# A two-layer decoder in one program: attention cores in chunks of four heads, and three-product scores and output projection in the second cross-attention

## The reference

```python
# self-attention, both layers (first cross-attention alike, no mask, keys of ctx: 1024)
scores = jnp.einsum('bhqd,bhkd->bhqk', q, k) / math.sqrt(dh)
scores = jnp.where(causal, scores, jnp.finfo(jnp.float32).min)
probs = jax.nn.softmax(scores, axis=-1)
attn = jnp.einsum('bhqk,bhkd->bhqd', probs, v)
...
# second cross-attention: H = 16 heads of D = 128, context split at N_IMG = 257
q = rms_norm(x @ q_w + q_b, nq_s).reshape(B, S, H, D)
k_txt = rms_norm(txt_ctx @ k_w + k_b, nkt_s).reshape(B, -1, H, D)
v_txt = (txt_ctx @ v_w + v_b).reshape(B, -1, H, D)
out_txt = sdpa(q, k_txt, v_txt)
k_img = rms_norm(img_ctx @ ki_w + ki_b, nki_s).reshape(B, -1, H, D)
v_img = (img_ctx @ vi_w + vi_b).reshape(B, -1, H, D)
out_img = sdpa(q, k_img, v_img)
out = (out_txt + out_img).reshape(B, S, INNER)
return out @ o_w + o_b
```

## Time and profile before

| | us |
|---|---|
| median of 3 runs | 3690.84 (3683.32 to 3691.17) |
| profiled execution: time | 3685.6 |
| profiled execution: span | 3683.8 |

### The profile page before, as it was taken

The page is one execution under the profiler, slowest core; times in us unless marked ns, Lnnn a source line. Parts: engine busy times, 40 slices in busy tenths (PEclk is TensorE's granted clock), DMA queues, the critical chain, the costliest instruction groups (busy, mean ns, idle before and its releaser), DMA issues. The chain is left out here.

```text
span 3683.8 us, 40622 instructions
## 1 busy us (share of the span) xinstructions
PE 3145.7 (85%) x13163; PEld 1907.7 (52%) x13166; DVE 1262.7 (34%) x1863; ACT 966.9 (26%) x2096; POOL 835.5 (23%) x819
## 2 busy tenths in 40 slices
PE   7699796988549786888996998999999856999997
PEld 3354342333548633446885884555554442777773
DVE  3133334564401212435434225555552131111114
ACT  1133033554101012323332004444442000222220
POOL 2100001100121101002442104555553013212215
PEclk9656897999669986659998999999999957999998
DMA  2132203331059612313443433222220000999996
GB/s 77 44 80 58 88 12 76 71 76 31 28 183 325 225 62 58 81 47 123 140 142 114 133 99 132 71 71 72 71 71 20 24 18 16 340 334 338 338 332 190
DMA packets 320633, 442.93 MB, mean 120 GB/s; under 512 B 45502, under 2 KB 179622, under 8 KB 320520
## 3 DMA queue, kind: packets, MB, share of 16 engines
q1 hardware_dynamic: 290056, 370.14, 32.4%
q0 software_dynamic: 15488, 44.09, 3.8%
q10 hardware_dynamic: 14976, 27.27, 2.1%
HBM read 308.78 MB, written 75.58 MB: 104 GB/s over the span
## 5 line engine op out<-in xcount | busy, mean ns | idle before, releaser
L1360 PE MATMUL ps<-moe_blocks_xgt,moe_blocks_w 128*128 128x128 f32 (+1 forms) x3072 | 364.0, 277 | 8.8 <-DMA moe_blocks_b1s<-rb_cols 5.5
L510 ACT ACTIVATE normed<-ps 128x512 f32<-128x512 f32 (+3 forms) x512 | 247.5, 516 | 463.7 <-PE ps L452 293.3
L1360 PEld LDWEIGHTS ps<-moe_blocks_xgt,moe_blocks_w 128*128 128x128 f32 (+1 forms) x3072 | 348.9, 183 | 16.6 <-issue 15.0
L2239 POOL TENSOR_TENSOR normed<-normed,xa_core_rinv 128x257 f32<-128x257 f32 (+1 forms) x256 | 266.2, 1062 | 273.0 <-DVE xa_core_rinv L2170 273.0
L1342 PE MATMUL ps<-moe_blocks_w,moe_blocks_ht 128*128 128x512 f32 (+1 forms) x624 | 284.9, 593 | 0.0
L2206 ACT ACTIVATE normed<-ps,xa_core_nmax 128x257 f32<-128x257 f32 (+1 forms) x256 | 173.8, 685 | 321.8 <-DVE xa_core_nmax L2165 321.4
L2116 PE MATMUL ps<-xa_core_k,xa_core_q 128*128 128x512 f32 x512 | 242.3, 596 | 14.1 <-DVE xa_core_k L2155 11.4
L2165 DVE TENSOR_REDUCE xa_core_nmax<-ps 128x1 f32<-128x257 f32 (+1 forms) x256 | 164.5, 683 | 250.1 <-PE ps L2116 250.1
L1431 DVE COPY moe_blocks_y<-ps 128x512 f32<-128x512 f32 x104 | 72.0, 692 | 459.9 <-PE ps L1342 436.3
L2142 PE MATMUL ps<-xa_core_pt,xa_core_v 128*128 128x512 f32 x512 | 225.1, 592 | 0.7 <-DVE xa_core_pt L2178 0.7
L559 DVE TENSOR_REDUCE xa_core_nmax<-ps 128x1 f32<-128x1024 f32 x128 | 156.0, 1224 | 139.9 <-PE ps L432 139.9
(11 more groups left out here) (290 smaller groups left out, 5263.7 us busy)
## 6 DMA issues: line engine op xcount, KB each, us to landing
moe_blocks_w<-L_ffn_rw SPq DMA_DIRECT2D x80, 704.0 KB
...
sa_core_packed<-sa_core_parts SPq DMA_DIRECT2D x384, 64.0 KB
...
```

What stands on the lines that cost most here:

```text
L510: nc.scalar.activation(probs[:, e % RING, a:S], g.ps[:, 4 + h, a:S], ACT.Exp).then_inc(exp_done, 1)
L1360: mm = nc.tensor.matmul(g.ps[0:fn, 2 + s % 2 + 2 * half, f * P:(f + 1) * P], w1s[s][:, k, half * F + f0:half * F + f0 + fn], xgt[:, s % 2, ...
L2239: ins = nc.gpsimd.tensor_tensor(prob[:, n % PR, lo:hi], prob[:, n % PR, lo:hi], rinv[:, n % PR, m:m + 1].to_broadcast([P, hi - lo]), ALU.mult)
```

## The change

`attention_core` works on NI = 8 chunks of four heads instead of 16 pairs. The high and low parts of a chunk go to DRAM in one DMA (`spill`), and six DMAs of 32 partitions x 4 heads bring them back packed (`pack`, 1.5 MB for a self-attention chunk, 2.25 MB for a cross-attention chunk); rows go in by two DMAs. The packed tensors have three slots (`pq`, `pk`). Values are stored plainly, [P, B, kt, D]; PE multiplies four heads of 32 columns into one bank and, with `g.ones`, the four sums into another, so that nothing has to be laid out: `lay` is gone, ACT takes both banks and DVE divides in the middle of the maxima of the next chunk. Both heads' score products now come ahead of both mask products. The maxima of chunk i + 1 are spread as EACH = 3 groups per key block of chunk i.

In the second cross-attention, keys are scaled by their gain at the projection (a second activation per unit), and queries are stored as high and low parts; the reciprocal for queries is one per token row (`rq` is [P, NT]) and comes into maximum and exponential as a scale. In the core GpSimd scales the keys, ACT and DVE split them, PE makes each score product as three float32r products (`split_matmul`) and a quarter of the values of the head before in every step. Keys have one raw buffer and are loaded ahead of the values. `output_cross1` is new: heads outside, the eight token tiles inside over eight banks, three products each.

```diff
-    NI, NP, QB = B * KC, B * KC * HPC // 2, S // P
-    NK = nkt * P
-    KB = NK // S
-    SLOTS = 4
+    NI, QB = B * KC, S // P
+    KB = nkt * P // S
+    SLOTS = 3
     PB = 2 if causal else 1
-    RING = 8
+    STEPS = 2
     TERMS = ((0, 0), (1, 0), (0, 1))
     KR = len(TERMS) * DH
-    PACK = 16 * 2 * 2 * len(TERMS)
+    PACK = 16 * 2 * len(TERMS)
+    PCS = HPC * QB // 2 if causal else HPC * QB
+    EACH = -(-PCS // (nkt - 1))
...
+            def spill(i):
+                sp.wait_ge(low_done, 2 * i + 2)
+                sp.dma_start(parts_dram[i], parts[i % PB][:, :, :].bitcast(F32)).then_inc(spilled[i % 2], 16)
+
+            def pack(i):
+                s = i % SLOTS
+                sp.wait_ge(spilled[i % 2], 16 * (i // 2 + 1))
+                if i >= SLOTS:
+                    sp.wait_ge(st_made, HPC * nkt * (i - SLOTS + 1))
+                t = parts_dram[i].rearrange("(h p) a n -> p h a n", p=DH)
+                for r, (qp, kp) in enumerate(TERMS):
+                    sp.dma_start(pq[r * DH:(r + 1) * DH, s, :, :].bitcast(F32),
+                                 t[:, :, qp, :]).then_inc(packed_in[s], 16)
+                    sp.dma_start(pk[r * DH:(r + 1) * DH, s, :, :].bitcast(F32),
+                                 t[:, :, 2 + KB * kp:2 + KB * (kp + 1), :].rearrange("p h a n -> p h (a n)")
+                                 ).then_inc(packed_in[s], 16)
+
+            def put_rows(i):
+                sp.wait_ge(row_low, i + 1)
                 for n in range(2):
-                    for h in range(2):
-                        sp.dma_start(packed[KR + n:KR + n + 1, j % SLOTS, h, 0, :].bitcast(F32),
-                                     rows[h * QB:(h + 1) * QB, j % 2, n, :].bitcast(F32)).then_inc(rows_in[j % 2], 16)
-
-            def lay(j):
-                i = j // 2
-                sp.wait_ge(taken, j + 1)
-                if j % 2 == 0 and i >= 1:
-                    sp.wait_ge(normed, i)
-                for h in range(2):
-                    a = (2 * (j % 2) + h) * DH
-                    val, ones = (3 if h else 0) * DH, (1 + h) * DH
-                    sp.dma_start(ot[a:a + DH, i, :], osb[val:val + DH, j % 2, :]).then_inc(spread[j % 2], 16)
-                    sp.dma_start(total[a:a + DH, :], osb[ones:ones + DH, j % 2, :]).then_inc(spread[j % 2], 16)
-
-            for j in range(SLOTS):
-                pack(j)
+                    sp.dma_start(pq[KR + n:KR + n + 1, i % SLOTS, :, :].bitcast(F32),
+                                 rows[:, i % 2, n, :].bitcast(F32)).then_inc(rows_in[i % 2], 16)
...
+            spill(0)
+            spill(1)
+            pack(0)
+            pack(1)
             put_rows(0)
-            for j in range(NP):
-                if j >= 1 and j + SLOTS - 1 < NP:
-                    pack(j + SLOTS - 1)
-                if j + 1 < NP:
-                    put_rows(j + 1)
-                if j >= 1:
-                    lay(j - 1)
-            lay(NP - 1)
-            for n in range(2):
-                sp.wait_ge(spread[n], 64 * NP // 2)
+            for i in range(NI):
+                if i + SLOTS - 1 < NI:
+                    spill(i + SLOTS - 1)
+                    pack(i + SLOTS - 1)
+                if i + 1 < NI:
+                    put_rows(i + 1)
...
+            def values(i, kb):
+                step, a = nkt * i + kb, start_of(kb)
+                b, c = divmod(i, KC)
+                pe.wait_ge(exp_done, HPC * step + HPC)
+                if kb == 0 and i >= 1:
+                    pe.wait_ge(taken, 2 * i)
+                for h in range(HPC):
+                    nc.tensor.matmul(g.ps[h * DH:(h + 1) * DH, 6, a:S], v[:, b, kb, c * P + h * DH:c * P + (h + 1) * DH],
+                                     probs[:, HPC * (step % STEPS) + h, a:S], start=(kb == 0), stop=(kb == nkt - 1))
+                for h in range(HPC):
+                    mm = nc.tensor.matmul(g.ps[h * DH:(h + 1) * DH, 7, a:S], g.ones[:, 0:DH],
+                                          probs[:, HPC * (step % STEPS) + h, a:S], start=(kb == 0), stop=(kb == nkt - 1))
+                mm.then_inc(pv_made, 1)
...
+            for i in range(NI):
                 for kb in range(nkt):
-                    scores(j, kb, 0)
-                    scores(j, kb, 1)
-                    if kb == 0 and j + 1 < NP:
-                        turn(j + 1)
+                    ahead = range(min(PCS, EACH * kb), min(PCS, EACH * (kb + 1))) if i + 1 < NI else ()
+                    if i == 0:
+                        for m in ahead:
+                            piece(i + 1, m)
+                    scores(i, kb, 0)
+                    if i > 0:
+                        for m in ahead:
+                            piece(i + 1, m)
+                    if kb == nkt - 1 and i + 1 < NI:
+                        turn(i + 1)
+                    scores(i, kb, 1)
                     if kb >= 1:
-                        values(j, kb - 1)
-                    elif j >= 1:
-                        values(j - 1, nkt - 1)
-                    if j + 2 < NP:
-                        piece(j + 2, kb)
-            values(NP - 1, nkt - 1)
+                        values(i, kb - 1)
...
+            def take(i):
+                act.wait_ge(pv_made, nkt * (i + 1))
+                if i >= 1:
+                    act.wait_ge(normed, i)
+                nc.scalar.activation(total[:, :], g.ps[:, 7, :], ACT.Copy).then_inc(taken, 1)
+                nc.scalar.activation(ot[:, i, :], g.ps[:, 6, :], ACT.Copy).then_inc(taken, 1)
...
+            for i in range(NI):
                 for kb in range(nkt):
-                    exp(j, kb, 0)
-                    exp(j, kb, 1)
-                    if kb == 0 and j + 1 < NP:
-                        row(j + 1)
-                    if kb == 1 and j >= 1:
-                        take(j - 1)
-                    if kb == nkt // 2 and j % 2 == 0 and j // 2 + 2 < NI:
-                        high_parts(j // 2 + 2)
-            take(NP - 1)
+                    exp(i, kb, 0)
+                    exp(i, kb, 1)
+                    if kb == nkt - 1 and i + 1 < NI:
+                        row(i + 1)
+                    exp(i, kb, 2)
+                    exp(i, kb, 3)
+                    if kb == 0 and i >= 1:
+                        take(i - 1)
+                    if kb == nkt // 2 and i + 2 < NI:
+                        high_parts(i + 2)
...
+            for i in range(NI):
+                for m in range(PCS if i + 1 < NI else 0):
+                    top(i + 1, m)
+                    if m == PCS // 2 and i >= 1:
+                        norm(i - 1)
...
+        @block.tensor
+        def _(pe):
+            for h in range(H):
+                pe.wait_ge(o_lows, h + 1)
+                pe.wait_ge(w_lows, h + 1)
+                r = h % RING
+                for t in range(NT):
+                    b, s = divmod(t * P, S)
+                    mm = split_matmul(nc, g.ps[:, t, :], o_high[:, r, b, s:s + P], o_low[:, r, b, s:s + P],
+                                      w_high[:, r, :], w_low[:, r, :], start=(h == 0), stop=(h == H - 1))
+                    if h == H - 1:
...
-                dst = rk[:, c * 512:(c + 1) * 512] if c < B * 2 else rq[:, (c - B * 2) * 512:(c - B * 2 + 1) * 512]
-                nc.vector.reciprocal(dst, rms[:, c % 2, :]).then_inc(inverted, 1)
+                nc.vector.reciprocal(rk[:, c * 512:(c + 1) * 512], rms[:, c % 2, :]).then_inc(inverted, 1)
+            dve.wait_ge(rooted, B * 2 + 1)
+            nc.vector.reciprocal(rq[:, :], rms_q[:, :]).then_inc(inverted, 1)
...
+                for c in range(0, CTX, 512):
+                    mm = split_matmul(nc, s_ps(n)[:, c:c + 512], q[:, s, 0, qs], q[:, s, 1, qs], k_high[:, s, c:c + 512],
+                                      k_low[:, s, c:c + 512], start=True, stop=True)
...
+            def step(i, n, b, nb):
+                multiply(i, n)
+                if reaches(i, n - SKEW - QB):
+                    values(i, n)
+                if reaches(i, n - SKEW):
+                    turn(i, n)
...
+                nc.vector.tensor_scalar(nmax[:, n % PR, :], peak[:, n % PR, :], rq[:, b * QB + n % QB:b * QB + n % QB + 1],
+                                        None, ALU.mult).then_inc(max_done, 1)
...
+                    ins = nc.scalar.activation(prob[:, n % PR, lo:hi], s_ps(n)[:, lo:hi], ACT.Exp,
+                                               bias=nmax[:, n % PR, m:m + 1], scale=rq[:, t:t + 1],
+                                               accum_out=rsum[:, n % PR, m:m + 1])
+                ins.then_inc(exp_done, 1)
...
+            def scale(j, b):
+                pool.wait_ge(k_loaded, 16 * j + 16)
+                nc.gpsimd.tensor_tensor(k[:, :], k[:, :], rk[:, b * CTX:(b + 1) * CTX], ALU.mult).then_inc(k_done, 1)
```

698 lines of the change are left out of this document (365 added, 333 removed).

## The result

The changed kernel takes 3808.12 us in the median of four runs (3807.69 to 3813.76) against 3689.86 for the kernel before; the ratio is 1.0328, 95% interval 1.031 to 1.0346. The forecast was 3684, and the top of the range 3768. The change costs 118 us, and the trace puts all of the loss into the three chunked cores: from the end of the projection ahead of them to the output projection they are 39, 126 and 42 us longer, 208 together, of which the second cross-attention gives back 86.

The account below looks back on a forecast made before the run. PE was busy most of the time, so its waits for rows behind packs decide. Terms 63 + 20 - 67 - 16 - 4 = -4 put the median 3690.8 at 3687; self-core startup made it 3684, range 3600 to 3768.

Parts of the forecast that it names:

- The second cross core: Second cross-attention core: three products and spread values, steps of 3.95 us, heads of 16.05 in place of 18.3; -67 us.
- the output projection: Output projection of the second cross-attention: 87.2 us of products, a lead of 3.5, 3 for slow clock; -16 us.
- keys and queries: Keys and queries of the second cross-attention: fewer reciprocals, -6.6 us, less possible PE waits of 3; -4 us.
- Rival (d): Second cross core stays near its waits, by alternation of kinds or a longer chain: +25 us, near 3710; chance 0.10.
- a chain of fixed length: Chunked cores: parts, spill, packs, then rows, behind the middle key block's exponential; 14.5 us self core, 18.4 cross core.
- first three members: Stretch to the exponential, parts, spill: self core 18, 3.7, 4.0 us; cross core 28.4 + 2.5, 5.3, 5.3.
- the term of the packs: Chunked cores, last part of the chain: packs and rows take 6.6 us in the self core, 7.7 in the cross core.
- Rival (b): Packs into 32 partitions go at the rate of today's, 220 GB/s: +63 us, 3747; chance 0.20.
- first cross core: First cross-attention core: periods of 49.3 us a chunk against 40.2, 984 us against 921; +63 us.
- Self core: Each self-attention core: periods of 32.5 us against 28.4, earlier start and shorter end; +10 us, +20 for both.
- Rival (c): Chunked cores: 32-column products not fully side by side; +68 us cross core, +34 self cores, near 3780; chance 0.12.
- The rule of ring order: Chunked cores: DMA engines take descriptors in ring order, so rows cannot pass packs; otherwise cross core 6 to 7 us less.

Follow-up runs that it names:

- the run with the third term apart: Changed kernel with the packs of the third term (partitions 64 to 95) issued from ScalarE's queue, the first two from SyncE's: 3807.79 us, single run beside 3678.

## Why the prediction was wrong

**What held.** The second cross core: a step was to be 3.95 us. The trace of the changed kernel, PE from one step's values to the next:

```profile
2602.56 1.88 PE L2223 MATMUL ps<-xa_core_pt,xa_core_v 128*128 128x512 f32 x4
2604.28 1.04 PE L2237 MATMUL ps<-identity,normed 128*128 128x128 f32 x8
2605.07 0.48 PE L1679 MATMUL ps<-xa_core_k_high,xa_core_q 128*128 128x512 f32 x1
...
2606.55 1.88 PE L2223 MATMUL ps<-xa_core_pt,xa_core_v 128*128 128x512 f32 x4
```

3.99 us, 16.0 a head against my 16.05; the core is 65 shorter (I said 67), the output projection 18 with its lead (16; the lead was 5.6 us and not 3.5), keys and queries 3 (4). Rival (d) did not come.

The mechanism of the cores held as well: a chain of fixed length behind ScalarE's middle exponential, with a wait for rows at each chunk and a slow clock behind it. Its first three members were right or near: 18.2 us to the exponential in the self core (18), 3.8 for the parts (3.7), 3.9 for the spill (4.0); in the cross core 32.8 (28.4 + 2.5), 1.9 a chunk too little, then 5.3 (5.3) and 5.1 (5.3). A key block with three groups of maxima takes 5.5 us, as I had it (777.68, 783.20, 788.70 in the changed kernel).

**What failed** is the term of the packs: 6.6 us in the self core measured 10.4, and 7.7 in the cross core measured 14.3, so that PE waited some 14.8 and 11.7 us a chunk for the rows where I had 12 and 5. I took the rate of a plain store, 390 GB/s, because the old packs read SBUF and the new ones DRAM. The row of the old packs was the nearer one, since it has the same destination, 32 partitions; by its share it gave 220 at full engines, and the packs run at 203 to 216. Rival (b) was what happened, and even its price was too small: in the six full chunks of the cross core 6.6 us each instead of 4.5, and in the self cores 3.8 instead of 3. (Where (b) is weighed, 31.5 MB at 390 GB/s are put at 81 us; with the MB used elsewhere they are 85. Nothing hangs on it.)

**The sum made again** from the same list: first cross core 63, and 7 for a later start of the scores (58.8 us from the core's start in place of 51.6), 50 for six periods of 57.7 in place of 49.3 (40 of them the packs, 11 the first member), 5 for the seventh chunk: 125 of the 126 measured. Self core 10, and 5 for the start, 20 for six periods of 35.8 in place of 32.5, 5 for the two last chunks: 40, where 39 and 42 were measured. Both edges of the range had the term in them too small: (b) was put at 3747, since the bound was the rate of the old packs and the tails of the cores were not in it.

**Clock and products.** Rival (c) was wrong. Four products of 32 columns side by side (PE, changed kernel):

```profile
781.35 1.06 PE L456 MATMUL ps<-normed,xa_v 128*32 128x512 f32 x8
782.23 1.04 PE L459 MATMUL ps<-normed,all_ones 128*32 128x512 f32 x8
783.20 0.72 PE L440 MATMUL ps<-xa_core_pq,xa_core_pk 98*128 98x512 f32 x2
```

Values and sums of a key block take 1.85 us in place of 2 x 1.01, close to the lower bound of 2 x 0.86. The rule of three column tiles in the Trainium skill, "TensorE: Matmul & The Clock Gate", section "Part 3: Packing small matmuls — row/col tiling", 2.38x and so short of the full factor, is not what these rows show for four: eight instructions in 0.88 and 0.97 us are 3.9 and 3.5 times faster than 8 x 0.43.

The rule of ring order (the Trainium skill, "DMA: Bandwidth & Descriptors", section "Queues, rings and completion order") speaks of descriptors on one engine; that the rows could not pass the packs was my inference from it. No run here sets it apart from another cause: rows alone on another queue, with nothing ahead of them in it, were as late as rows behind the packs.

**What stays open**: why transfers into 32 partitions stop at 200 GB/s. The write side is likely in the cross core after the run with the third term apart, but its rate came to 253 and not to twice 200, in the self cores it did not rise at all, and nothing was run that changes the source alone.
